# Causal attention with 8-wide heads: masking the turned exponentials on GpSimd instead of adding the mask on TensorE

## The reference

```python
scale = np.float32(1.0 / np.sqrt(D))               # D = 8, T = 256, H = 16
q = _heads(x @ Wq + bq)
k = _heads(x @ Wk + bk)
v = _heads(x @ Wv + bv)
att = jnp.einsum('bhqd,bhkd->bhqk', q, k) * scale
causal = jnp.tril(jnp.ones((T, T), bool))
att = jnp.where(causal[None, None], att, -jnp.inf)
y = jnp.einsum('bhqk,bhkd->bhqd', jax.nn.softmax(att, axis=-1), v)
```

## Time and profile before

| | |
|---|---|
| median of 3 runs | 3069.31 us (3066.16 to 3073.21) |
| the profiled execution's own time | 3067.32 us |
| its span in the trace | 3065.6 us |
| PE busy / DVE / ACT / POOL, share of the span | 73% / 67% / 38% / 41% |
| the stage `l1s`, first turned scores to last exponential | about 505 to 833 us of the span |

### The profile page before, as it was taken

The page is one execution under the profiler, slowest core; times in us unless marked ns, Lnnn a source line. Parts: engine busy times, 40 slices in busy tenths (PEclk is TensorE's granted clock), DMA queues, the critical chain, the costliest instruction groups (busy, mean ns, idle before and its releaser), DMA issues. The chain is left out here.

```text
span 3065.6 us, 68634 instructions
## 1 busy us (share of the span) xinstructions
PE 2242.5 (73%) x22154; PEld 1627.9 (53%) x22154; DVE 2055.0 (67%) x5574; ACT 1149.7 (38%) x2369; POOL 1251.0 (41%) x1958
## 2 busy tenths in 40 slices
PE   4823996999876247499999476994678888887633
PEld 2523994666554236377777354663445555555412
DVE  4843554666578446488887565775648888877786
ACT  2401552333333036255555333442223333333344
POOL 3444324555243555577776312322313322323211
PEclk9955997999989579799999787996759999998855
DMA  6021111000000112100000000000001111100000
GB/s 261 1 102 43 54 54 27 13 12 14 7 1 26 57 57 78 43 12 10 9 10 6 8 4 14 0 1 7 1 26 45 42 49 44 41 31 3 12 1 28
DMA packets 81039, 96.22 MB, mean 31 GB/s; under 512 B 16354, under 2 KB 60268, under 8 KB 78764
## 3 DMA queue, kind: packets, MB, share of 16 engines
q1 hardware_dynamic: 72628, 76.73, 7.8%
q0 software_dynamic: 8192, 16.79, 1.8%
HBM read 56.12 MB, written 37.36 MB: 30 GB/s over the span
## 5 line engine op out<-in xcount | busy, mean ns | idle before, releaser
L1780 ACT ACTIVATE l2f_experts_h<-l2f_experts_f,l2f_experts_bias 128x512 f32<-128x512 f32 x256 | 176.4, 689 | 286.5 <-DVE l2f_experts_h_lo L1841 239.2
L1841 DVE TENSOR_TENSOR l2f_experts_h_lo<-l2f_experts_h,l2f_experts_h_hi 128x512 fp32r<-128x512 f32 x256 | 250.3, 978 | 8.7
L1875 POOL TENSOR_TENSOR l2f_acc<-l2f_experts_tmp,l2f_acc 128x512 f32<-128x512 f32 x64 | 89.8, 1403 | 339.1 <-DVE l2f_experts_tmp L1808 339.1
L883 POOL TENSOR_TENSOR a_pm<-a_pt,tri_post 128x256 f32<-128x256 f32 x256 | 179.9, 733 | 94.6 <-ACT a_pt L543 94.5
L678 DVE TENSOR_REDUCE l1s_negm<-l1s_s 128x3 bf16<-128x384 f32 x256 | 131.3, 557 | 108.0 <-PE l1s_s L380 107.1
L678 DVE TENSOR_REDUCE a_negm<-a_s 128x2 bf16<-128x512 f32 x256 | 164.7, 686 | 33.9 <-PE a_s L380 32.5
L1705 PE MATMUL l2f_experts_y<-l2f_experts_h_hi,l2f_experts_w_hi 128*128 128x512 f32 x256 | 126.3, 494 | 49.4 <-DVE l2f_experts_h_lo L1841 33.8
L543 ACT ACTIVATE l1s_pt<-l1s_st 128x768 f32<-128x768 f32 x128 | 96.9, 812 | 157.6 <-PE l1s_st L415 157.6
L1705 PEld LDWEIGHTS l2f_experts_y<-l2f_experts_h_hi,l2f_experts_w_hi 128*128 128x128 f32 x256 | 48.1, 188 | 156.0 <-DVE l2f_experts_h_lo L1841 113.6
L543 ACT ACTIVATE a_pt<-a_st 128x1024 f32<-128x1024 f32 x128 | 126.2, 1061 | 2.8 <-PE a_st L415 2.8
L1839 DVE CAST l2f_experts_h_hi<-l2f_experts_h 128x512 fp32r<-128x512 f32 x256 | 112.5, 439 | 13.7 <-ACT l2f_experts_h L1780 13.7
(11 more groups left out here) (527 smaller groups left out, 6962.9 us busy)
## 6 DMA issues: line engine op xcount, KB each, us to landing
expert_rows<-zeros SPq DMA_DIRECT2D x16, 1056.0 KB, 17.0
l2f_experts_wrow<-weights_by_expert SPq DMA_DIRECT2D x64, 256.0 KB, 3.1
l0f_w<-in_l0f_w SPq DMA_DIRECT2D x8, 640.0 KB
l0f_x_in_sb<-expert_rows SPq DMA_DIRECT2D x72, 64.0 KB, 1.8
expert_rows<-l0f_y SPq DMA_DIRECT2D x72, 64.0 KB, 1.6
l1f_x_in_sb<-expert_rows SPq DMA_DIRECT2D x72, 64.0 KB, 1.8
expert_rows<-l1f_y SPq DMA_DIRECT2D x72, 64.0 KB, 1.6
l2f_experts_raw<-in_l2f_w SPq DMA_DIRECT2D x8, 512.0 KB, 4.6
```

Of the source, the lines that this page charges most:

```text
L883: last = pool.tensor_tensor(pm[:, par, heads_, kt, :], pt[:, par, heads_, kt * (T + P):kt * (T + P) + P], K["tri_post"][:].unsqueeze(1).br ...
L1780: act.activation(h[:, j], psum_f[j][:], ACT.Gelu, bias=col(e, j)).then_inc(h_ready, 1)
L1841: dve.tensor_tensor(h_lo[:, pos % 2, j], h[:, j], h_hi[:, pos % 2, j].bitcast(F32), ALU.subtract)\
L1875: pool.tensor_tensor(acc[:, bass.ds(c * CH, CH)], tmp[:, pos % 2], acc[:, bass.ds(c * CH, CH)], ALU.add).then_inc(added, 1)
```

## The change

For `causal="before"`, `shift` no longer adds `mask_k`. Instead GpSimd clears, after each of the two exponentials of a unit, the part of `pt` where the key is after the query, in place, by one `affine_select` over four blocks of 128 columns (two heads, two diagonal blocks). `pt` gets a row of 512 instead of 384 columns per head, so that the four blocks are at equal distance. `values` waits for both selects. `score_mask` and with it `mask_q` stay.

```diff
-        pt = sb("pt", [P, 2, 4, SC])
+        pt = sb("pt", [P, 2, 4, 2 * T if before else SC])
...
             def shift(n, pos):
                 if before:
-                    for i in range(4):
-                        pe.matmul(psum_st[:, i, :].rearrange("p (j k) -> p j k", j=2)[:, :, 0:P], K["ident_bf"][:],
-                                  K["mask_k"][:, 0:1, 0:P].broadcast_to([P, 2, P]), start=False, stop=False,
-                                  skip_group_check=True)
                     pe.wait_ge(max_joined, n + 1)
...
-                if pm is not None:
+                if causal:
                     pe.wait_ge(pm_ready, 2 * n + 2)
...
-                act.activation(pt[:, pos % 2, 2 * g:2 * g + 2, :], psum_st[:, 2 * g:2 * g + 2, 0:SC], ACT.Exp,
+                act.activation(pt[:, pos % 2, 2 * g:2 * g + 2, 0:SC], psum_st[:, 2 * g:2 * g + 2, 0:SC], ACT.Exp,
...
+            def select(n, pos, g):
+                pool.wait_ge(exp_done, 2 * n + 1 + g)
+                pool.sem_inc(K["passed"], 1)
+                blocks = pt[:, pos % 2, 2 * g:2 * g + 2, :].rearrange("p h (j k) -> p h j k", j=2)[:, :, :, 0:P]
+                pool.affine_select(out=blocks, in_=blocks, compare_op=ALU.is_ge, fill=0.0, base=0,
+                                   pattern=[[0, 2], [0, 2], [1, P]], channel_multiplier=-1).then_inc(pm_ready, 1)
...
-                if pm is not None and inside(n):
-                    mask(n, pos, 0)
-                    mask(n, pos, 1)
+                if causal and inside(n):
+                    for g in range(2):
+                        select(n, pos, g) if before else mask(n, pos, g)
```

## The result

The changed kernel took 3085.41 us (median of 4 runs, 3081.87 to 3089.18), the kernel before 3067.73 us beside it (4 runs): 17.7 us more. The ratio is 1.0057, with a 95% interval of 1.0036 to 1.0079, so it is slower by more than the 0.2% that can be told apart. The profiled execution has a span of 3082.1 us, 16.5 above that of before.

A forecast was written before the change was run, and what follows sets the result against it. TensorE, though 92% busy, was taken to wait for VectorE's join at most unit ends. Removal 0, selects hidden, held joins about 8 us: 3067.3 + 8 = 3075.3, plus 2.0 for the runs' median gives 3077 us; range 3065 to 3091.

The forecast's parts named there:

- What bounds the kernel: Units follow the loop shift, scores, maxima, scores, maxima, join; TensorE waits for VectorE's join, and the masks lie in its shadow.
- The select's duration: 128 selects on GpSimd at 0.62 us each, upper bound 0.87; 79 us in all, GpSimd then 243 of 328 us busy.
- `values` never waits for a select: `values` stands on TensorE behind the next `shift`, which waits for the join, so the new wait costs nothing.
- The joins: Moved GpSimd work meets VectorE's joins: 0.6 us per batch (0.26 to 1.1), 7.8 us over 13 batches, about 0.5 for the rest.
- the middle between slipping in and waiting for both key products: Join ending unit 1 meets `kb_hi` and `kb_f`: +0.06 if in between, +0.47 if it waits for both; +0.25 taken.
- the forecast's +0.2: Join ending unit 0 meets the gather's second half: +0.13, up to +0.35 if merges push it; +0.2 taken.
- A slip of the prediction: In unit 3 the gather was put at 672.45, 0.36 before the join at 672.81, which might slip through; +0.15 us taken.
- The removal: Taking the masks off TensorE gains 0, bounds 0 and 16 x 0.31 = 5.0 us, where unit 2 passes to 3.
- The argument from the mean share: TensorE, 261 of some 336 us busy, keeps full clock, since the next stage has it at 79% busy.
- The forecast's own case: GpSimd's moved work holds joins: +8 us, reaching from +3.4 to +15; chance 0.57.
- the rival in which GpSimd sets the pace with slow selects: Selects of 0.87 us make key products late in units 0, 1 and 3: 1.5 us x 13 = 20, 3090 us; chance 0.12.

The follow-up runs named there:

- e2_neither: Changed kernel without the selects and their waits, so the turned scores are not masked at all: +2.1 us against the kernel before, ratio 1.0004.
- e8_no_mask_q_before: Kernel before with the join as a one-input reduction and without the `mask_q` matmuls, `mask_k` kept: 22.8 us faster than before, ratio 0.9927.
- e1_mask_and_select: Changed kernel with the four `mask_k` matmuls per unit put back beside the selects: +11.2 us against the kernel before, ratio 1.0034.
- e7_no_mask_q_select: Changed kernel with the join as a one-input reduction and without the `mask_q` matmuls: 18.7 us faster than the kernel before, ratio 0.9937.
- e3_after_reduce_join: Changed kernel with the join written as a one-input reduction into its own slot: +3.0 us against the kernel before, ratio 1.0009.
- e10_reduce_join_again: Changed kernel with the one-input join, run once more on another chip: +0.8 us against the kernel before, ratio 1.0004.
- e5_select_last: Changed kernel with the two selects moved to the end of GpSimd's unit, behind the key products: +47.6 us against the kernel before, ratio 1.0158.
- e6_after_again: The changed kernel, unaltered, run once more on another chip: +14.9 us against the kernel before, ratio 1.0045.

## Why the prediction was right in sign and too small

*What bounds the kernel.* Right. Removing 39 us of matmuls shortened nothing (e2_neither, +2.1 us), and removing matmuls that lie in the loop did (e8_no_mask_q_before, -22.8 us).

*The select's duration.* Right: 0.64 us against 0.62, so f32 in four runs has no price of its own, and GpSimd doesn't set the pace. That `values` never waits for a select was right for 63 units. The last one waited 1.4 us, and the stage's end came 0.9 us later: the argument had leaned on a next `shift`, and the last unit has none.

*The joins.* The mechanism and its sum were right. I had 0.6 us per batch and 8.3 in all; e1_mask_and_select, which differs from before by the selects alone, has 8.9 us in the stage. Unit by unit the sum was distributed otherwise. Ahead of unit 2, where I took the middle between slipping in and waiting for both key products, it waits for both: 0.64, and the joins there follow each other by 0.47 us more. Ahead of unit 1 it is 0.25 or 0.34 by turns, near the 0.36 that the forecast's +0.2 makes. Ahead of unit 0 the gather had begun 0.57 us before the join (594.50, 595.07), not 0.36, so the join was held (0.42), little more than before. A slip of the prediction plays in here: selects that end at 670.98, 1.20 us of `vb` and the 0.15 us between `vb` and the gather in the earlier trace rows give a gather from 672.33, 0.48 before the join, and not from 672.45. At 0.48 its own rows had a held join. That a gather doesn't hold such an instruction, as the Trainium skill's page "SBUF — State Buffer" infers in the section named in the prediction, is contradicted again by the joins at 595.07 and 600.15 above.

*The removal: 0, with bounds from 0 to 5.0 us of gain.* This is the step that failed, by its bounds. It had no side on which taking matmuls away costs time. The two profiles of the changed kernel are 5.9 and 6.6 us longer in the stage than e1_mask_and_select, which has the same joins and selects, and differs by the masks alone. In the first, 2.1 us of it lie between the first three joins (5.89 + 6.92 us against 5.78 + 4.90), and 3 x 1.3 us at the three places inside the stage (6.69 + 6.06 us for two units, otherwise 5.58 + 5.89). So the term of the removal, forecast as 0, measured about 6 us of loss. I named the clock as what would make the prediction wrong and set against it the next stage, at 79% busy and 1.00. The changed stage is 80% busy and loses its clock all the same, while e7_no_mask_q_select keeps it with less:

```profile
565.00:770.00 205.00, 157.02 (x2288) 112.34 (x2288) 142.27 (x375) 81.82 (x135) 170.45 (x283) 1.00 0.05 14
```

That is 77% busy at 1.00. The argument from the mean share was the mistake: it did not tell these stages apart.

*How the two losses go together.* Places of lost clock are counted here after the stage's third join. With masks and held joins (e1_mask_and_select) there is none. Without masks and without newly held joins (e2_neither, e3_after_reduce_join, e10_reduce_join_again, e7_no_mask_q_select) there is none either. Without masks and with held joins there are three in the changed kernel, each time, and 13 in e5_select_last, where the joins are held longest. So inside the stage it takes both. The masks filled some 0.6 us ahead of each `shift`; without them TensorE idles from the end of the turned scores to the end of the join, 1.14 us at 605.85 where the join is held, and 42.7 us over the stage, against 8.8 us before. Idle time of this kind is not enough: e2_neither has 34.6 us of it and no place inside. That the longer idle time ahead of one `shift` is what tips the clock fits all these kernels, but is argued and not shown by itself. Why it happens behind three of the nine held joins of this kind, and of the ten in e6_after_again, stays open.

*The size.* 8 us were forecast, 17.7 measured, 14.9 the second time. Joins 8.9 and clock 6 make 15 between the first and the last join, and 0.9 lie at the stage's end. The rest, up to 1.8 us, is less than the runs tell.

*The range.* That 3085 us lies within 3065 to 3091 is partly luck. The forecast's own case reached to +15 us, and 17.7 is beyond that. The range went further only for the rival in which GpSimd sets the pace with slow selects, and that did not happen. No case of the prediction had the cause that filled the gap.

## What to carry to other kernels

Work that is taken off an engine which is 92% busy gains nothing if it lay beside the operation that the engine waits for anyway; look at what the first instruction behind it follows. Work that is put on GpSimd is paid where VectorE has a short instruction with two SBUF inputs on the critical path. Once that instruction was written with one input (here a reduction over both operands in one tile), the same GpSimd work cost 2 us by the profiles, less than the runs could tell. At the end of a stage, look at what no longer has other work to hide it. And matmuls that cost no time may still be what keeps TensorE's clock, so removing them can cost time.

## What the runs showed of the hardware

A VectorE instruction of two SBUF inputs can wait for more than one GpSimd instruction: 1.65 us instead of 0.16 in e5_select_last, through three that followed each other without a gap. It need not: in the changed kernel the join at 513.85 took 0.46 us and ended at 514.31, with `kb_hi` (513.65 to 514.28), although `kb_f` had followed from 514.22. What decides between the two was not found. TensorE went to the 1.2 GHz level inside a stage in which it was 80% busy, after an idle time of 1.14 us ahead of `shift`; it was back at full clock within the same unit, and this unit and the next took 1.3 us more. The same idle time at 562.83 had no such effect.
